# Scores and score maxima of two attention blocks in sixteen 32x32 parts of the array instead of four of 32x128

## The chip, the cores and the metric

The kernel runs on one core of one Trainium2 chip. The metric is the device time of one execution in microseconds (us), and lower is better. The reference gives the result in 32-bit floats; the kernel uses 32-bit matmuls for everything that enters the result and bf16 matmuls where only a maximum or a mask is wanted.

## The reference

Four stages, one after the other, on x of 4 batches x 512 rows x 256 features, with a context of 4 x 1601 x 256:

```
x = x + tanh(g_xattn[0]) * cross_attention(layernorm(x), ctx)          # 16 heads of 64, 1601 keys
x = x + tanh(g_ffn[0])  * attention_and_experts(layernorm(x))          # 16 heads of 16, 4 key heads, 512 keys
x = x + tanh(g_xattn[1]) * masked_attention(ctx, ctx, layernorm(x))    # 16 heads of 16, 1601 keys, masked
x = x + tanh(g_ffn[1])  * attention_plus_gated_experts(layernorm(x))   # 16 heads of 16, 512 keys
```

Each attention is a softmax over keys of query times key, and that softmax times values. The third stage adds a mask of -1e20 to the scores before the softmax:

```
energy = jnp.einsum('nqhd,nkhd->nhqk', q, k)
energy = jnp.where(mask == 0, jnp.float32(-1e+20), energy)
attn = jax.nn.softmax(energy / math.sqrt(EMBED), axis=3)
out = jnp.einsum('nhql,nlhd->nqhd', attn, v)
```

## The kernel before

The kernel calls the four stages blocks 1 to 4. Blocks 2, 3 and 4 have heads of 16 features. Such a head is laid out in a strip of 32 partitions (`PAD` = 32: one row for minus the maximum, 16 for the features, the rest zero), and a group is four heads, one strip each. There are 4 groups (`GROUPS`) in each of 4 batches.

For a group, these units of work follow each other:

- **Score maxima.** `max3` (block 3) and `maxb` (blocks 2 and 4) take a tile of 128 queries and two heads. Per head there is one bf16 matmul: its stationary operand is 32 rows (the strip) x 128 queries, its moving operand 32 rows x 401 keys (block 3) or 512 keys. The two heads lie in different row strips of the array and in different banks. VectorE then reduces both banks to maxima (L1679 for block 3, L1689 for blocks 2 and 4). Block 3 has 4 query tiles x 4 key chunks x 2 head pairs = 32 units a group, 512 in all, written at L1228. Block 4 has 8 units a group, 128 in all, written at L1240, as are those of block 2.
- **Scores.** `scoreb` takes a tile of 124 keys (block 3, 13 tiles) or 128 keys (blocks 2 and 4, 4 tiles), and all four heads of the group. Per head there is one 32-bit matmul at L1267: stationary 32 rows x 128 keys, moving 32 rows x 512 queries. The compiled program runs each 32-bit matmul as two passes, so that a unit has 8 MATMUL records. Heads 0 and 1 go to a first slot of two banks, heads 2 and 3 to a second one, which has its own wait (`second_free`). In block 3 two full-array bf16 matmuls lay the mask under heads 0 and 1 before (L1260), and two add it to heads 2 and 3 behind (L1273). ScalarE takes the exponentials of each slot (L1435). Block 3 has 208 such units, block 4 has 64, and block 2 has 64.
- **Values.** `pvb` (L1288) multiplies the exponentials by the values: per head one 32-bit matmul in two passes, stationary 124 or 128 rows x 32 columns, moving 512 queries. The four heads lie in different column strips.

Three slots of two banks (`ring`, `RING` = 3) hold everything but the sums over values. `pv` has two banks. The order of the units is fixed: eight streams are woven together by a written list of turns (`TURNS_1` for blocks 1 and 2, `TURNS_3` for blocks 3 and 4), and a planner (`Pace`) gives each unit its slot from costs written in the code. In the second weave the order alternates `max3`, `pvb`, `maxb` or an expert of block 4, `scoreb`. TensorE works through this one list. Each unit waits for its slot and its inputs through semaphores, and only the last matmul of a unit (and, in `scoreb`, the last one of head 1) counts up `tensor_done`.

Of the kernel before, what the change touches and what calls it, by code (L numbers as in the profile page):

```python
# [15 lines left out]
P = 128  # L16
BANK = 512
# [5 lines left out]
PAD = P // GROUP  # L23
# [4 lines left out]
CHUNK = 401  # L28
# [4 lines left out]
GROUPS = HEADS // GROUP  # L33
# [723 lines left out]
def flamingo(nc, t, out):  # L757
# [3 lines left out]
    with ctx:  # L761
# [166 lines left out]
        def key_columns(blk, g, k0):  # L928

            if blk == 3:  # L930
                return kq_3[:, (g % 2) * (CTX + S) + k0:(g % 2) * (CTX + S) + k0 + P]
            return keys_place(blk, g)[:, k0:k0 + P]

        def queries_place(blk, g):
            if blk == 3:
                return kq_3[:, (g % 2) * (CTX + S) + CTX:(g % 2 + 1) * (CTX + S)]
            if blk == 2:
                return kq_2[:, g * S:(g + 1) * S]
            return kq_4[:, (g % 2) * 2 * S:(g % 2) * 2 * S + S]
# [6 lines left out]
        def queries_low(blk, g):  # L946
            return {2: kq_2b[:, g * S:(g + 1) * S], 3: kq_3b[:, CTX + 1:CTX + 1 + S], 4: kq_4b[:, 0:S]}[blk]
# [30 lines left out]
        def head_bank(unit, h):  # L978
            return ring_t[:, bank_of[unit][h // 2], (h % 2) * BANK:(h % 2 + 1) * BANK]
# [94 lines left out]
        def _(pe):  # L1074
            past = Past(pe)
            past.wait_ge(*at("vector", "setup"))
            for unit in order:
# [9 lines left out]
                slot = None  # L1087
                if unit in bank_of:
                    for lane, other in plan.bank_free[unit]:
                        past.wait_ge(*at(lane, *other))  # L1090
                    slot = slot_tile(unit) if kind != "scoreb" else None
                if kind == "turn":
                    blk, b = a
                    xn = xn_a if blk == 1 else xn_of[blk] if blk in xn_of else src[:, b, :, :]
                    source = ("rms1", b) if blk == 20 else ("ln", blk, b)
                    for q in range(QT):
                        past.wait_ge(vector_done, plan.end["vector", source] - QT + 1 + q)
                        for f in range(FT):
                            last = pe.transpose(slot[:, f * S + q * P:f * S + (q + 1) * P], xn[:, q, f * P:(f + 1) * P], ident)
                    last.then_inc(tensor_done, 1)  # L1100
                elif kind == "kproj":
# [3 lines left out]
                    for j in range(2):  # L1105
                        c0 = CTX_CHUNKS[2 * c + j]
                        place = slot[:, j * BANK:j * BANK + CHUNK]
                        pe.matmul(place, pair_weights(p)[:, 1, 0, :], ctxT[:, 0, c0:c0 + CHUNK], start=True, stop=False)  # L1108
                        last = pe.matmul(place, pair_weights(p)[:, 1, 1, :], ctxT[:, 1, c0:c0 + CHUNK], start=False, stop=True)  # L1109
                    last.then_inc(tensor_done, 1)  # L1110
                elif kind == "qproj":
# [5 lines left out]
                              start=False, stop=True).then_inc(tensor_done, 1)  # L1117
                elif kind == "vproj":
                    b, p, j = a
                    for i, (k0, kn) in enumerate(CTX_TILES[8 * j:8 * j + 8]):  # L1120
                        place = slot[0:kn, i * P:(i + 1) * P]
                        pe.matmul(place, ctxT[:, 0, k0:k0 + kn], pair_weights(p)[:, 2, 0, :], start=True, stop=False)  # L1122
                        last = pe.matmul(place, ctxT[:, 1, k0:k0 + kn], pair_weights(p)[:, 2, 1, :], start=False, stop=True)  # L1123
                    last.then_inc(tensor_done, 1)
                elif kind == "maxa":
                    b, p, q, c = a
                    c0 = CTX_CHUNKS[c]
                    past.wait_ge(*at("vector", "qproj", b, p))
                    for h in range(2):
                        own = slice(64 * h, 64 * h + 64)  # L1130
                        last = pe.matmul(slot[:, h * BANK:h * BANK + CHUNK], queries_ab[own, q * P:(q + 1) * P],  # L1131
                                         keys_ab[own, c0:c0 + CHUNK], start=True, stop=True)
                    last.then_inc(tensor_done, 1)
                elif kind == "rowa":
                    b, p = a
                    past.wait_ge(*at("vector", "nega", b, p))
                    for q in range(QT):
                        last = pe.matmul(slot[:, q * P:(q + 1) * P], neg_cols_a[:, q, :], ident_b[:, :], start=True, stop=True)
                    last.then_inc(tensor_done, 1)
                elif kind == "scorea":  # L1140
                    b, p, k = a
                    k0, kn = CTX_TILES[k]
                    past.wait_ge(*at("scalar", "qproj", b, p))
                    past.wait_ge(*at("scalar", "rowa", b, p))
                    for h in range(2):
                        own = slice(64 * h, 64 * h + 64)
                        pe.matmul(slot[:, h * BANK:(h + 1) * BANK], select_b[own, :], neg_rows[own, p % 2, :], start=True, stop=False)  # L1147
                    for h in range(2):
                        own = slice(64 * h, 64 * h + 64)
                        last = pe.matmul(slot[0:kn, h * BANK:(h + 1) * BANK], keys_a[own, p % 2, k0:k0 + kn], queries_a[own, p % 2, :],  # L1150
                                         start=False, stop=True)
                    last.then_inc(tensor_done, 1)
                elif kind == "pva":
# [6 lines left out]
                    for h in range(2):  # L1160
                        last = pe.matmul(pv_a[64 * h:64 * h + 64, :], values_a[0:kn, p % 2, k, 64 * h:64 * h + 64],  # L1161
                                         exps_a[0:kn, slot_of["scorea", b, p, k], h * S:(h + 1) * S], start=k == 0, stop=k == NKT - 1)
# [26 lines left out]
                elif kind == "projqk":  # L1189
                    b, g = a  # L1190
# [31 lines left out]
                elif kind == "max3":  # L1222
                    b, g, q, hp, c = a
                    past.wait_ge(*at("dma", "load_low", b, g))
                    past.wait_ge(*at("vector", "low", b, g))
                    for i in range(2):
                        own = slice(PAD * (2 * hp + i), PAD * (2 * hp + i + 1))
                        last = pe.matmul(slot[:, i * BANK:i * BANK + CHUNK], queries_low(3, g)[own, q * P:(q + 1) * P],  # L1228
                                         keys_low(3, g)[own, CTX_CHUNKS[c]:CTX_CHUNKS[c] + CHUNK], start=True, stop=True)
                    last.then_inc(tensor_done, 1)  # L1230
                elif kind == "maxb":
# [3 lines left out]
                        past.wait_ge(*at("vector", "projq", b, g // 2))  # L1235
                    else:
                        past.wait_ge(*at("vector", "projqk", b, g))
                    for i in range(2):
                        own = slice(PAD * (2 * hp + i), PAD * (2 * hp + i + 1))
                        last = pe.matmul(slot[:, i * BANK:(i + 1) * BANK], queries_low(blk, g)[own, q * P:(q + 1) * P],  # L1240
                                         keys_low(blk)[own, :], start=True, stop=True)
                    last.then_inc(tensor_done, 1)
                elif kind == "rowb":
# [5 lines left out]
                elif kind == "scoreb":  # L1249
# [12 lines left out]
                    for h in range(GROUP):  # L1262
                        own = slice(PAD * h, PAD * h + PAD)
                        if h == 2:
                            for lane, other in plan.second_free[unit]:
                                past.wait_ge(*at(lane, *other))
                        last = pe.matmul(head_bank(unit, h), key_columns(blk, g, k0)[own, :],  # L1267
                                         queries_place(blk, g)[own, :], start=blk != 3 or h >= 2, stop=blk != 3 or h < 2)
                        if h == 1:
                            last.then_inc(tensor_done, 1)  # L1270
                    if blk == 3:
# [686 lines left out]
```

## Time and profile before

| what | value |
|---|---|
| three runs | 3416.55, 3425.77, 3425.16 us (median 3425.16) |
| span of the profiled execution, first to last instruction | 3413.1 us |
| TensorE busy | 3262.7 us (96%), 18335 MATMUL records |
| VectorE busy | 1980.1 us (58%) |
| ScalarE busy | 1437.7 us (42%) |
| GpSimd busy | 955.6 us (28%) |

The profiled execution has no time of its own beside its span; the three runs lie 3.5 to 12.7 us above the span, which leaves out what comes before the first and behind the last instruction. Busy TensorE time is from the start of a matmul to the modelled end of its results, and matmuls overlap in the array, so the 96% do not say that the array could take no more. What a unit costs is read from starts, not from busy times.

### The profile page before, as it was taken

Reading aid. Unit: us, or ns where it says so; the run is one execution under the profiler, and the core shown is the slowest. Engines: PE = TensorE matmul, PEld = TensorE weight load, DVE = VectorE, ACT = ScalarE, POOL = GpSimd, SP = SyncE. Lnnn points to the kernel's source line nnn. Section 1 sums busy time; section 2 is a strip of 40 time slices with the busy share of each in tenths; the row PEclk is TensorE's granted clock in tenths of the full one; section 3 lists DMA queues with packets and bytes.
Section 4 is the critical chain, followed back from the end, with each engine's and each line's share of the span. In section 5 each row is a group of like instructions: output and inputs, shape, how many; then the busy total and the mean of one; then the engine's idle time right before and its main releaser. Section 6 shows DMA issues by size and latency. Waiting matters only on the chain.

```text
span 3413.1 us, 45107 instructions
## 1 busy us (share of the span) xinstructions
PE 3262.7 (96%) x18335; PEld 1412.6 (41%) x18335; DVE 1980.1 (58%) x4290; ACT 1437.7 (42%) x1645; POOL 955.6 (28%) x469
## 2 busy tenths in 40 slices
PE   7999999999999999999997979899999999999999
PEld 3444444444434444444433752223333334333344
DVE  4444456554555546655574028677777676766446
ACT  3433444445434454344443213454444444545533
POOL 4655555654466444546300001000000000000000
PEclk9999999999999999999998989999999999999989
DMA  3000000000000000000031510211111111110000
GB/s 151 12 13 13 31 11 11 7 12 32 7 21 12 13 28 12 19 13 7 4 110 54 165 56 19 58 50 53 20 31 37 47 29 41 30 40 20 13 19 19
DMA packets 68249, 114.41 MB, mean 34 GB/s; under 512 B 4849, under 2 KB 49545, under 8 KB 67530
## 3 DMA queue, kind: packets, MB, share of 16 engines
q1 hardware_dynamic: 62666, 96.58, 8.9%
q0 software_dynamic: 5376, 14.95, 1.9%
q8 instruction: 144, 2.36, 0.3%
q14 instruction: 63, 0.52, 0.0%
HBM read 101.30 MB, written 16.78 MB: 35 GB/s over the span
## 4 chain that ended last, share of the span: by engine, by line
PE 85%; DVE 6%; ACT 4%; POOL 2%; DMA 1%; issue 1%; ACTq 0%; DVEq 0%; POOLq 0%
PE pv L1161 11%; PE ring L1267 10%; PE ring L1150 9%; PE pv L1288 9%; PE ring L1228 3%; PE ring L1260 3%; PE ring L1131 3%; PE ring L1122 3%; PE ring L1108 3%; PE ring L1147 3%; PE ring L1123 3%; PE ring L1109 2%; PE ring L1273 2%; ACT wide L1435 2%; PE ring L1345 2%; PE ring L1326 2%
## 5 line engine op out<-in xcount | busy, mean ns | idle before, releaser
L1532 POOL TENSOR_TENSOR wide<-wide 124x1024 f32<-124x1024 f32 (+1 forms) x341 | 803.6, 2357 | 180.1 <-ACT wide L1428 142.1
L1435 ACT ACTIVATE wide<-ring 124x1024 f32<-124x1024 f32 (+2 forms) x544 | 528.3, 1022 | 532.2 <-PE ring L1267 529.7
L1651 DVE TENSOR_REDUCE max_a<-ring 128x2 f32<-128x802 f32 x512 | 493.3, 990 | 395.9 <-PE ring L1131 395.6
L1428 ACT ACTIVATE wide<-ring 124x1024 f32<-124x1024 f32 (+1 forms) x416 | 425.0, 1026 | 438.3 <-PE ring L1150 386.0
L1679 DVE CUSTOM_DVE_ANT_0 rest<-ring,slim 128x401 bf16<-128x401 f32 x683 | 374.5, 575 | 119.4 <-PE ring L1228 113.5
L1150 PE MATMUL ring<-wide 64*124 64x512 f32 (+1 forms) x1664 | 424.8, 589 | 0.0
L1161 PE MATMUL pv<-wide 124*64 124x512 f32 (+1 forms) x1664 | 414.0, 613 | 8.2 <-ACT wide L1428 8.2
L1689 DVE TENSOR_REDUCE slim<-ring 128x2 f32<-128x1024 f32 x256 | 307.9, 1221 | 111.2 <-PE ring L1240 109.4
L1267 PE MATMUL ring<-slim 32*128 32x512 f32 x2176 | 350.5, 641 | 3.4 <-ACT wide L1435 2.7
L1502 POOL DMA_DIRECT2D slim<-in_ctx_k x16 | 8.9, 560 | 988.4 <-PE ring L1228 938.0
L1529 POOL TENSOR_TENSOR wide<-wide 124x1024 f32<-124x1024 f32 x31 | 73.0, 2355 | 600.4 <-ACT wide L1428 587.0
L1679 DVE CUSTOM_DVE_ANT_0 slim<-ring,slim 128x401 bf16<-128x401 f32 x341 | 195.7, 574 | 67.1 <-PE ring L1228 65.5
L1288 PE MATMUL pv<-wide,slim 124*32 124x512 f32 (+1 forms) x1664 | 223.4, 610 | 0.2 <-ACT wide L1435 0.2
L1161 PEld LDWEIGHTS pv<-wide 124*64 124x64 f32 (+1 forms) x1664 | 99.3, 136 | 229.7 <-issue 201.9
L1150 PEld LDWEIGHTS ring<-wide 64*124 64x124 f32 (+1 forms) x1664 | 155.5, 183 | 72.9 <-issue 50.4
L1228 PE MATMUL ring<-slim 32*128 32x401 bf16 x1024 | 159.7, 341 | 21.2 <-ACT wide L1435 11.9
L1267 PEld LDWEIGHTS ring<-slim 32*128 32x128 f32 x2176 | 112.3, 184 | 133.4 <-issue 104.8
L1147 PE MATMUL ring<-wide,select_b 64*128 64x512 bf16 x832 | 158.9, 379 | 8.1 <-ACT wide L1428 6.1
L1131 PE MATMUL ring<-wide 64*128 64x401 bf16 x1024 | 155.7, 337 | 9.5 <-DVE max_a L1651 4.5
L1122 PE MATMUL ring<-wide 128*124 128x128 f32 (+1 forms) x832 | 162.1, 276 | 0.4 <-DVE max_a L1651 0.4
L1123 PE MATMUL ring<-wide 128*124 128x128 f32 (+1 forms) x832 | 160.4, 273 | 0.0
L1435 ACT ACTIVATE slim<-ring 128x1024 f32<-128x1024 f32 x128 | 124.4, 1021 | 75.4 <-PE ring L1267 75.0
(241 smaller groups left out, 3992.1 us busy)
## 6 DMA issues: line engine op xcount, KB each, us to landing
slim<-in_ctx_k SPq DMA_DIRECT2D x16, 800.5 KB, 4.4
wide<-in_w_pair SPq DMA_DIRECT2D x32, 384.0 KB, 3.1
slim<-in_ctx_v SPq DMA_DIRECT2D x16, 744.0 KB
wide<-in_w SPq DMA_DIRECT2D x16, 512.0 KB, 4.9
wide<-in_we SPq DMA_DIRECT2D x16, 512.0 KB, 3.7
wide<-in_ctxT SPq DMA_DIRECT2D x4, 1601.0 KB, 7.0
slim<-in_ctx_k POOLq DMA_DIRECT2D x16, 400.2 KB, 4.7
wide<-padded_x SPq DMA_DIRECT2D x8, 640.0 KB, 5.2
```

Source lines behind the costliest of these rows:

```text
L1122: pe.matmul(place, ctxT[:, 0, k0:k0 + kn], pair_weights(p)[:, 2, 0, :], start=True, stop=False)
L1123: last = pe.matmul(place, ctxT[:, 1, k0:k0 + kn], pair_weights(p)[:, 2, 1, :], start=False, stop=True)
L1150: last = pe.matmul(slot[0:kn, h * BANK:(h + 1) * BANK], keys_a[own, p % 2, k0:k0 + kn], queries_a[own, p % 2, :], start=False, stop=True)
L1161: last = pe.matmul(pv_a[64 * h:64 * h + 64, :], values_a[0:kn, p % 2, k, 64 * h:64 * h + 64], exps_a[0:kn, slot_of["scorea", b, p, k], h * ...
L1267: last = pe.matmul(head_bank(unit, h), key_columns(blk, g, k0)[own, :], queries_place(blk, g)[own, :], start=blk != 3 or h >= 2, stop=blk ...
L1288: last = pe.matmul(pv_of[blk][PAD * h:PAD * h + PAD, :], value_columns(blk, g, k, kn, h), exps_tile(blk, b, g, k, h)[0:kn, :], start=k == ...
L1428: sc.activation(exps_a[0:kn, slot_of[unit], :], slot[0:kn, :], ACT.Exp, scale=WIDE ** -0.5).then_inc(scalar_done, 1)
L1435: sc.activation((exps_2 if blk == 2 else exps_34)[0:kn, first + 2 * i:first + 2 * i + 2, :].rearrange("p h n -> p (h n)"), ring_t[0:kn, ba ...
L1532: po.tensor_tensor(sums[0:kn, :], sums[0:kn, :], view, ALU.add).then_inc(pool_done, 1)
L1651: ve.reduce_max(max_a[:, :, q, c], slot.rearrange("p (h n) -> p h n", h=2)[:, :, 0:CHUNK], AX.X).then_inc(vector_done, 1)
L1679: ve.tensor_tensor_reduce(out=max_junk[junk], in0=slot[:, i * BANK:i * BANK + CHUNK], in1=maskQ_sb[:, q, CTX_CHUNKS[c]:CTX_CHUNKS[c] + CHUNK],
L1689: ve.tensor_reduce(neg_cols[blk][:, q, 2 * hp * PAD:2 * hp * PAD + PAD + 1:PAD], slot.rearrange("p (h n) -> p h n", h=2), AX.X, ALU.max, n ...
```

## The change

In block 3 and block 4 each matmul of `scoreb` and of the maxima is cut into four along its 128 stationary columns. Each part has 32 rows and 32 columns, writes 32 partitions of the same bank, and streams the same moving operand as the others of its head. Block 2 keeps matmuls of 32x128. Data, order of the units, slots, waits and semaphore counts stay as they were. In the `scoreb` of block 2 the loop runs once.

```
                 elif kind == "max3":
...
-                    for i in range(2):
+                    for i, j in product(range(2), range(GROUPS)):
                         own = slice(PAD * (2 * hp + i), PAD * (2 * hp + i + 1))
-                        last = pe.matmul(slot[:, i * BANK:i * BANK + CHUNK], queries_low(3, g)[own, q * P:(q + 1) * P],
+                        last = pe.matmul(slot[j * PAD:(j + 1) * PAD, i * BANK:i * BANK + CHUNK],
+                                         queries_low(3, g)[own, q * P + j * PAD:q * P + (j + 1) * PAD],
                                          keys_low(3, g)[own, CTX_CHUNKS[c]:CTX_CHUNKS[c] + CHUNK], start=True, stop=True)
                     last.then_inc(tensor_done, 1)
                 elif kind == "maxb":
...
-                    for i in range(2):
-                        own = slice(PAD * (2 * hp + i), PAD * (2 * hp + i + 1))
-                        last = pe.matmul(slot[:, i * BANK:(i + 1) * BANK], queries_low(blk, g)[own, q * P:(q + 1) * P],
+                    for i, j in product(range(2), range(1 if blk == 2 else GROUPS)):
+                        own, wide_part = slice(PAD * (2 * hp + i), PAD * (2 * hp + i + 1)), P if blk == 2 else PAD
+                        c0 = j * wide_part
+                        last = pe.matmul(slot[c0:c0 + wide_part, i * BANK:(i + 1) * BANK],
+                                         queries_low(blk, g)[own, q * P + c0:q * P + c0 + wide_part],
                                          keys_low(blk)[own, :], start=True, stop=True)
                     last.then_inc(tensor_done, 1)
...
-                        last = pe.matmul(head_bank(unit, h), key_columns(blk, g, k0)[own, :],
-                                         queries_place(blk, g)[own, :], start=blk != 3 or h >= 2, stop=blk != 3 or h < 2)
+                        wide_part = P if blk == 2 else PAD
+                        for c0 in range(0, P, wide_part):
+                            last = pe.matmul(head_bank(unit, h)[c0:c0 + wide_part, :], key_columns(blk, g, k0)[own, c0:c0 + wide_part],
+                                             queries_place(blk, g)[own, :], start=blk != 3 or h >= 2, stop=blk != 3 or h < 2)
                         if h == 1:
                             last.then_inc(tensor_done, 1)
```

## Rows read from the trace of the kernel before

**Rows 1.** The profile's page: busy time, granted clock in 40 slices, chain by engine
```profile
PE 3262.7 (96%) x18335; PEld 1412.6 (41%) x18335; DVE 1980.1 (58%) x4290; ACT 1437.7 (42%) x1645; POOL 955.6 (28%) x469
...
PEclk9999999999999999999998989999999999999989
...
PE 85%; DVE 6%; ACT 4%; POOL 2%; DMA 1%; issue 1%; ACTq 0%; DVEq 0%; POOLq 0%
```

**Rows 2.** Windows by stage: stretch, length, busy us of each engine, clock, DMA
```profile
0.00:1940.00 1940.00, 1859.99 (x10212) 872.48 (x10213) 1022.19 (x1452) 809.02 (x955) 916.06 (x422) 0.98 0.09 31
2040.00:3200.00 1160.00, 1122.39 (x6681) 384.18 (x6680) 829.06 (x2611) 530.27 (x574) 31.66 (x39) 0.98 0.14 35
```

**Rows 3.** Groups of TensorE instructions from 2075 us to the end
```profile
L1267 PE MATMUL ring<-slim 32*128 32x512 f32 x1664 | 268.3, 643 | 2.7 <-ACT wide L1435 2.7
L1288 PE MATMUL pv<-wide,slim 124*32 124x512 f32 (+1 forms) x1664 | 223.4, 610 | 0.2 <-ACT wide L1435 0.2
L1228 PE MATMUL ring<-slim 32*128 32x401 bf16 x960 | 148.8, 342 | 20.6 <-ACT wide L1435 11.9 <-DVE max_b L1679 5.5 <-DVE slim L1710 1.5
...
L1267 PE MATMUL ring<-wide 32*128 32x512 f32 x512 | 82.6, 638 | 2.0 <-ACT wide L1457 0.9 <-DVE max_b L1679 0.5 <-DVE wide L1704 0.2
```

**Rows 4.** Chain of waits, 2600 to 2640 us: first and last of eight L1267 pieces
```profile
2601.31 1.47 PE ring L1267 x8
...
2610.20 1.07 PE ring L1267 x8
...
2635.49 1.40 PE ring L1267 x8
```

**Rows 5.** Timeline, second weave: start us, length, engine, line
```profile
2600.70 0.61 PE L1260 MATMUL ring<-slim,ident_b 124*128 124x512 bf16 x2
...
2601.24 1.54 PE L1267 MATMUL ring<-slim 32*128 32x512 f32 x8
...
2602.71 0.61 PE L1273 MATMUL ring<-slim,ident_b 124*128 124x512 bf16 x2
...
2603.25 0.34 PE L1228 MATMUL ring<-slim 32*128 32x401 bf16 x2
...
2603.52 1.06 PE L1288 MATMUL pv<-wide,slim 124*32 124x512 f32 x8
...
2604.52 0.59 PE L1228 MATMUL ring<-slim 32*128 32x401 bf16 x6
...
2610.13 1.14 PE L1267 MATMUL ring<-slim 32*128 32x512 f32 x8
```

**Rows 6.** Timeline of TensorE, window 2604.4 to 2604.6 us
```profile
2603.98 0.61 PE L1288 MATMUL pv<-wide,slim 124*32 124x512 f32 x4
2604.52 0.35 PE L1228 MATMUL ring<-slim 32*128 32x401 bf16 x4
```

**Rows 7.** Instructions of single lines: duration ns min/median/max
```profile
L1267 PE MATMUL ring<-slim x2176: 587/588/1218, 523.3 to 3265.7; 32*128 32x512 f32 x198
...
L1288 PE MATMUL pv<-wide,slim x1664: 590/594/1063, 2086.4 to 3273.5; 124*32 124x512 f32 x170, 113*32 113x512 f32 x15
...
L1228 PE MATMUL ring<-slim x1024: 325/339/513, 2042.1 to 3195.5; 32*128 32x401 bf16 x171
```

**Rows 8.** Timeline of TensorE: neighbours of two shapes in blocks 1 and 2
```profile
946.60 1.02 PE L1150 MATMUL ring<-wide 64*124 64x512 f32 x4
947.55 0.87 PE L1240 MATMUL ring<-slim 32*128 32x512 bf16 x4
...
703.02 1.08 PE L1161 MATMUL pv<-wide 124*64 124x512 f32 x4
704.03 1.06 PE L1288 MATMUL pv<-slim 128*32 128x512 f32 x8
```

**Rows 9.** Timeline of TensorE, 1384.8 to 1385.2 us: first and last of 14 short matmuls
```profile
1384.84 0.17 PE L1334 MATMUL ring<-chosen_b,earlier_b 128*128 128x8 bf16 x1
...
1385.17 0.17 PE L1337 MATMUL ring<-before_b,ones_b 128*128 128x8 bf16 x1
```

## The prediction

> **What bounds the kernel now.** I read the page first. TensorE is busy for 96% of the span, the next engine, VectorE, for 58%, and 85% of the chain that ended last is TensorE's [rows 1]. The clock row is nearly all 9s: outside the gap between the two weaves the granted clock is the upper level, 2.4 GHz, and the change leaves no longer pauses, so I count no clock effect. The windows place the change. Blocks 3 and 4 fill the time from 2040 us to the end; up to 3200 us TensorE is busy for 1122 of 1160 us, VectorE for 829 and ScalarE for 530 [rows 2]. The groups from 2075 us on show that TensorE hardly waits in front of the changed lines: 2.7 and 2.0 us ahead of the scores, 20.6 us ahead of the block 3 maxima [rows 3]. In this stage a nanosecond added between two matmul starts is therefore paid almost in full, and one saved is kept almost in full.
>
> Busy time says little of a unit's cost, since a matmul's record holds a tail that overlaps the next one. I read starts. A merged row of the timeline gives its first start and its length; the length less one matmul's own duration is the time from first to last start.
>
> **How an unchanged scores unit runs.** The undisturbed unit is eight records in 1.14 us [rows 5]; one lasts 0.588 us [rows 7], so the last starts 0.55 us after the first. A 512-column bf16 matmul takes 0.61 - 0.39 = 0.22 us of starts (the mask pair at 2600.70 [rows 5]); a pass of a 32-bit matmul takes two of those, 0.43 us, as the pair of 64-row heads at 946.60 shows (1.02 - 0.59) [rows 8]. So the L1267 unit has 0.12 us beside its pass. Four starts of L1288 lie in 0.61 - 0.594 = 0.02 us, 0.0065 us apart [rows 6, 7]; four heads take 0.02 us of the 0.12. The other 0.10 us is the load of the second pass's 128 weight columns, which is not hidden here. L1288, with 32 columns, has 1.06 - 0.594 = 0.47 us from first to last start [rows 5, 7]: 0.02 of starts and 0.03 of load. L1161, with 64 columns, lies between [rows 8].
>
> **What the change costs, part by part.**
>
> 1. *Scores, 208 + 64 = 272 units (1664/8 and 512/8 records [rows 3]).* Removed: 128-column loads; added: 24 more records and as many loads a unit. If sixteen parts load side by side, as L1288's four column parts and L1267's four row strips do, the exposed load falls from 0.10 to 0.03 us. The starts grow from three intervals to fifteen, 15 x 0.0065 = 0.10 us in place of 0.02. Last start: 0.43 + 0.03 + 0.10 = 0.56 us against 0.55. I take the unit as unchanged. No row shows 32x32 parts. The load is bounded by zero (the 946.60 row exposes none) and by four loads one after the other in a strip, 4 x 0.03 = 0.11 us: -0.03 to +0.08 us a unit, -8 to +22 us in all. A unit's 32 matmuls and 32 loads must also be fed in one go, and the rows show bursts of eight only. I add 0.01 us a unit, 3 us, for feeding, with 0 below.
>
> 2. *Scores whose second half waits.* Of eight L1267 pieces of the chain between 2600 and 2640 us three take 1.07 us and five longer, up to 1.51 [rows 4]; the 1.54 us unit at 2601.24 is such a one, its heads 2 and 3 waiting for their slot [rows 5]. There the end is the second half's start plus its own length, which falls from 0.54 us (0.43 + 0.10 + one interval) to 0.43 + 0.03 + 7 x 0.0065 = 0.50. With half of 272 units: 136 x 0.04 = -5.5 us. A gain of nothing is the other bound.
>
> 3. *Maxima, 512 + 128 = 640 units.* The four starts of L1228 at 2604.52 lie in 0.35 - 0.339 = 0.01 us, some 0.0035 us apart [rows 6, 7]. Eight starts in place of two put the last one 6 x 0.0035 = 0.02 us later, and what comes behind in another shape waits for the last. In the cycle shown L1228 is followed by L1288 0.27 us after its start [rows 5], so this is on the path. Full count: 640 x 0.02 = +13 us. Some units overlap with another of the same shape or wait for a slot, so I take two thirds, +9 us. At the spacing of the 32-bit starts it would be 640 x 0.04 = +25 us.
>
> 4. *Maxima in the same strips again.* In the six-record row at 2604.52 the third pair starts 0.59 - 0.34 = 0.25 us after the first [rows 5], where 401 columns at 2.4 GHz are 0.17: 0.08 us of load is exposed, and 0.03 would be left. I estimate 50 such places, since most units come singly or as the two different head pairs: -2.5 us.
>
> 5. *Changes of shape.* L1260's second matmul starts at 2600.92 (2600.70 + 0.61 - 0.39) and streams for 0.21 us, the next shape starts at 2601.24: 0.1 us is left, and every change in the rows costs about that: full array to 32x128 [rows 5], 32x128 to 128x32 (0.27 less 0.17), 128x32 back, 64x128 to 32x128 and 128x64 to 128x32 [rows 8]. The last two keep the column or the row division and pay all the same. 32x32 beside 128x32 keeps the column division, so I expect 0.1 us there too, and no number of changes differs: block 3 and 4 have no 32x128 left beside.
>
> 6. *The others.* VectorE learns of its maxima 0.02 us later; it has slack [rows 2]. ScalarE may start heads 0 and 1 about 0.04 us sooner. DMA and its queues are untouched; SyncE's and GpSimd's reloads wait for the last maxima, whose drift is part of the sum.
>
> The Trainium skill speaks against the maxima's edit: "TensorEngine Tiling (Array Packing)", Restrictions and Gotchas, says that column tiling shuts off the fast weight load, which bf16 weights of 128 columns otherwise have. By that rule and the page "TensorE: Matmul & The Clock Gate" (LDWEIGHTS), 32 columns would load in an estimated 0.027 us against 0.08 in the row; the rule then costs nothing, unless the four loads queue (0.11), where term 4 would turn from -2.5 to +1.5 us.
>
> **Sum.** 0 + 3 - 5.5 + 9 - 2.5 = +4 us on a span of 3413.1. The runs lie 3.5 to 12.7 us above that span, their median 12.1; moved to the median, 3425.2 + 4 = **3429 us**. That is within 0.3% (10 us), about what a measurement of this kernel can tell from no change.
>
> **Rivals.**
>
> - *Loads of a strip's parts queue* (slower). In favour: no row shows more than four loads at once, and each strip has one stream of partitions. Against: L1288 loads four column parts together over all rows. Term 1 becomes +22, term 2 about zero, term 4 +1.5: 22 + 3 + 9 + 1.5 = +35 us, 3460. Chance 0.13.
> - *Too many parts for what can wait* (slower). A second pass waits in front of the next head's first pass in the program. With 16 parts, if only eight second passes can be held, heads 2 and 3 start when the first pass of 0 and 1 ends: +0.43 us where the second half doesn't wait anyway, 136 to 272 units, +58 to +117 us, 3490 to 3545. It decides from the ninth part on. L1267's row of eight shows that four can be held. Chance 0.07.
> - *Issue becomes the bound* (slower). Fourteen short matmuls start 0.33/13 = 0.025 us apart [rows 9]. Were that the price of each small matmul, a scores unit would need 32 x 0.025 = 0.80 us (+0.25, 67 us) and a maxima unit 0.17 more (110 us): about 3605. For scores it decides from 0.55/32 = 0.017 us a record. Against: parts start 0.0035 and 0.0065 us apart when in different tiles [rows 6]. Chance 0.04. The skill's "TensorE: Matmul & The Clock Gate", Back-to-back issue gap, has the same 25 ns as floor and, in one setting of the decoder, some 62 ns a matmul; the 0.025 us row and the closer starts speak against the latter.
> - *Going to and from the values becomes cheap* (faster), because 32x32 and 128x32 divide the columns alike. 2176/8 = 272 values units, entered and left: at most 544 x 0.1 = 54 us; with most neighbours of these shapes, 45 us less: 3384. Against it the changes in [rows 8]. Chance 0.10.
> - *The second pass's load vanishes*, as in the 64-row strips: 0.03 x 272 = 8 us less and the halves 4 us less: -8 us, 3417. Chance 0.10.
>
> **Chances and range.** The forecast has 0.56 and its own range is 3419 to 3441 (term 3 from two thirds to the wide spacing, feeding 0 to 6 us, term 2 absent or there). Faster by over 0.3%: 0.10 + 0.06 of the last rival + 0.03 of the forecast's low end = 0.19. Slower: 0.13 + 0.07 + 0.04 + 0.13 of the forecast's upper end = 0.37. Within: 0.44. The range runs from the cheap change of shape to the queued loads, 3380 to 3462, and leaves out some 0.12 above.
>
> **What would show it.** In the profile after: undisturbed scores units still near 1.14 us from first start to last end, and a first-to-second-pass distance of 0.46 us in place of 0.53 (queued loads: 0.53 or more; too many parts: heads 2 and 3 starting 0.43 us late). L1228 to L1288 0.29 us in place of 0.27. L1288 to the next shape still 0.1 us beyond its stream. The records of L1228 and L1267 four times as many. The prediction is wrong if sixteen parts don't stream together, which no row can tell, or if a change of shape is priced by more than the rows show.

## The result and the profile after

The changed kernel takes 3435.51 us, the median of 7 runs (3428.97 to 3438.61); the kernel before took 3425.16 us in 7 runs beside it (3416.55 to 3430.69). The ratio is 1.0034 with a 95% interval of 1.0023 to 1.0045. On 3425.16 us that is +11.6 us, between +8 and +15: slower. Whether it lies beyond the 0.3% that I took as the bound can't be told: the interval includes it, and the medians are 10.35 us apart, which is 0.30%. The profiled execution took 3428.97 us, its span 3426.8. Of the executions below, one of e7 and one each of the kernel before beside e5 to e7 and beside e8 and e9 fell into a much slower state of the chip and count in no figure.

The page of the kernel after. Against [rows 1] TensorE has 10,347 matmul records more and about the same busy time, and the clock row is again nearly all 9s:

```profile
PE 3270.1 (95%) x28682; PEld 1390.7 (41%) x28703; DVE 1982.4 (58%) x4290; ACT 1436.6 (42%) x1645; POOL 955.3 (28%) x469
...
PEclk9999999999999999999988989999999999999999
...
PE 85%; DVE 6%; ACT 4%; POOL 2%; issue 1%; DMA 1%; ACTq 0%; POOLq 0%; DVEq 0%
```

The windows of the stages in the kernel after, columns as in [rows 2]:

```profile
0.00:1940.00 1940.00, 1859.26 (x10195) 872.91 (x10204) 1023.06 (x1452) 808.71 (x955) 915.96 (x422) 0.98 0.09 31
2040.00:3200.00 1160.00, 1118.15 (x15756) 359.40 (x15762) 822.90 (x2586) 523.25 (x567) 31.64 (x39) 0.99 0.14 36
```

The first stretch is as before. In the second, VectorE does 2586 instructions where it did 2611 and ScalarE 567 where it did 574: the same length of time holds less work. The groups of TensorE from 2075 us on, kernel after. L1267 has become L1272, L1288 is L1293, L1240 is L1242, L1260 is L1263 and L1273 is L1278. ScalarE's L1435 is now L1440, and VectorE's L1679 and L1689 are L1684 and L1694:

```profile
L1272 PE MATMUL ring<-slim 32*32 32x512 f32 x6656 | 264.7, 606 | 2.8 <-ACT wide L1440 2.8
L1293 PE MATMUL pv<-wide,slim 124*32 124x512 f32 (+1 forms) x1664 | 223.1, 609 | 0.2 <-ACT wide L1440 0.2
L1228 PE MATMUL ring<-slim 32*32 32x401 bf16 x3872 | 162.9, 341 | 23.7 <-ACT wide L1440 14.7 <-DVE max_b L1684 6.0 <-DVE slim L1715 1.5
...
L1272 PE MATMUL ring<-wide 32*32 32x512 f32 x2048 | 81.9, 599 | 2.1 <-ACT wide L1462 0.9 <-DVE max_b L1684 0.5 <-ACT wide L1440 0.3
...
L1242 PE MATMUL ring<-wide 32*32 32x512 bf16 x1024 | 52.0, 395 | 4.2 <-DVE slim L1694 1.4 <-ACT wide L1440 1.1 <-DVE wide L1771 1.0
```

Set against [rows 3], the scores' busy time fell (268.3 to 264.7 and 82.6 to 81.9 us) and the maxima's rose (148.8 to 162.9 us). The idle time ahead of L1228 rose from 20.6 to 23.7 us.

The timeline of TensorE in the second weave, kernel after:

```profile
2604.33 0.60 PE L1263 MATMUL ring<-slim,ident_b 124*128 124x512 bf16 x2
2604.86 1.14 PE L1272 MATMUL ring<-slim 32*32 32x512 f32 x32
2605.93 0.60 PE L1278 MATMUL ring<-slim,ident_b 124*128 124x512 bf16 x2
2606.46 0.36 PE L1228 MATMUL ring<-slim 32*32 32x401 bf16 x8
2606.76 1.07 PE L1293 MATMUL pv<-wide,slim 124*32 124x512 f32 x8
2607.75 0.36 PE L1228 MATMUL ring<-slim 32*32 32x401 bf16 x8
2608.03 0.41 PE L1242 MATMUL ring<-wide 32*32 32x512 bf16 x8
...
2612.17 0.65 PE L1228 MATMUL ring<-slim 32*32 32x401 bf16 x24
```

Narrow windows of the same timeline, around 2605.58 us and up to 2605.25 us. They cut the 32 records into their two passes, second pass first:

```profile
2605.31 0.69 PE L1272 MATMUL ring<-slim 32*32 32x512 f32 x16
...
2604.86 0.71 PE L1272 MATMUL ring<-slim 32*32 32x512 f32 x16
```

The weight loads (PEld) of the same unit, kernel after:

```profile
2604.85 0.23 PEld L1272 LDWEIGHTS ring<-slim 32*32 32x32 f32 x32 [0.42 <-issue]
```

and the loads, the first pass and the second pass of the undisturbed unit in the kernel before:

```profile
2610.13 0.31 PEld L1267 LDWEIGHTS ring<-slim 32*128 32x128 f32 x8 [0.42 <-issue]
...
2610.13 0.71 PE L1267 MATMUL ring<-slim 32*128 32x512 f32 x4
...
2610.66 0.61 PE L1267 MATMUL ring<-slim 32*128 32x512 f32 x4
```

What the reader is to see here:

- The undisturbed scores unit lasts 1.14 us with 32 records, as it did with 8 [rows 5]. Its second pass starts 2605.31 - 2604.86 = 0.45 us after the first. All sixteen second passes lie in the first row, so its sixteen starts take 0.69 - 0.588 = 0.10 us, 0.0065 us apart.
- The load that the unit waits for is that of its first pass. The loads of both passes end at 2604.85 + 0.23 = 2605.08 us, 0.23 us before the second pass starts, and in the kernel before at 2610.44, 0.22 us before. It is the first pass whose records are longer: 0.71 - 0.02 = 0.69 us with 128 columns and 0.71 - 0.10 = 0.61 with 32, against 0.588 in the second pass. Their starts are recorded together with their loads, and the difference, 0.10 and 0.02 us, is what the load holds up.
- L1228 to L1293 takes 2606.76 - 2606.46 = 0.30 us, in place of 0.27 [rows 5]. The unit's own row grew from 0.34 to 0.36 us: that is the 0.02 us of later last start, and it comes out again behind the unit.
- Three maxima units in a row take 0.65 us in place of 0.59 [rows 5]. That is 0.06 us more for three units, and nothing came back.
- L1293 to the next L1228 takes 0.99 us, as L1288 to L1228 did before (1.00 us [rows 5]), although both now have column parts of 32.

Single instructions of L1228 in the kernel after (duration in ns, min/median/max):

```profile
L1228 PEld LDWEIGHTS ring<-slim x4096: 86/88/98, 2044.0 to 3207.9; 32*32 32x32 bf16 x196
L1228 PE MATMUL ring<-slim x4096: 324/339/513, 2044.1 to 3207.9; 32*32 32x401 bf16 x196
```

The pieces of the chain of waits at L1272, kernel after, 2600 to 2640 us:

```profile
2604.93 1.07 PE ring L1272 x32
...
2608.98 1.43 PE ring L1272 x27
...
2637.50 1.07 PE ring L1272 x32
```

Four of its eight pieces take 1.07 us, the length that the undisturbed unit had in [rows 4]; the long one shown takes 1.43 us, where the same unit took 1.47 before.

**Where the 11.6 us arise.** I compared the starts of the same instructions in the two traces. The changed kernel is 2.0 us late when the second weave begins, 4.0 us at 2133 us, 8.1 at 2637, 11.8 at 3142 and 13.7 at the end: the loss grows through the whole second weave. The 2.0 us arise before it, where TensorE's matmuls are those of the kernel before. Taken unit by unit, from a unit's first start to that of the next unit, the second weave says who pays. The 512 `max3` units cost +15.9 us and the 128 block 4 `maxb` units +2.2. The 208 `scoreb` units of block 3 cost -3.7 and the 64 of block 4 -0.7. Everything else comes to -2, and the sum is +11.7. It is the 13.7 us between two single executions less those 2.0; that it meets the 11.6 of the runs is chance. What is firm in it is the small, regular part. Of the 18.1 us at the maxima, 13.4 are shifts of at most 0.15 us. In 357 places a maxima unit stands alone between units of other kinds; the median shift there is +0.021 us, and only 3% of them move by less than 0.008 us. The other 5 us are single longer steps. Those come and go from one execution to the next: the traces of e1 and e4 to e7 below, whose maxima are whole as before, have 2 to 10 us more than before at the same units.

### The profile page after: what moved, and what is told of

Read it like the earlier page. It is cut to its first block, busy times and chain, and to the rows that moved or that the text cites. A ratio compares the mean times of both kernels' runs of the same rounds, so it can differ in the third digit from the quotient of the medians.

```text
span 3426.8 us, 65822 instructions
## 1 busy us (share of the span) xinstructions
PE 3270.1 (95%) x28682; PEld 1390.7 (41%) x28703; DVE 1982.4 (58%) x4290; ACT 1436.6 (42%) x1645; POOL 955.3 (28%) x469
## 4 chain that ended last, share of the span: by engine, by line
PE 85%; DVE 6%; ACT 4%; POOL 2%; issue 1%; DMA 1%; ACTq 0%; POOLq 0%; DVEq 0%
PE pv L1161 11%; PE ring L1272 10%; PE ring L1150 9%; PE pv L1293 9%; PE ring L1228 4%; PE ring L1263 3%; PE ring L1131 3%; PE ring L1122 3%; PE ring L1108 3%; PE ring L1147 3%; PE ring L1123 3%; PE ring L1109 2%; PE ring L1278 2%; ACT wide L1440 2%; PE ring L1350 2%; PE ring L1242 2%
## 5 line engine op out<-in xcount | busy, mean ns | idle before, releaser
L1440 ACT ACTIVATE wide<-ring 124x1024 f32<-124x1024 f32 (+2 forms) x544 | 527.5, 1021 | 543.4 <-PE ring L1272 541.7
L1684 DVE CUSTOM_DVE_ANT_0 rest<-ring,slim 128x401 bf16<-128x401 f32 x683 | 375.3, 576 | 124.4 <-PE ring L1228 121.6
L1694 DVE TENSOR_REDUCE slim<-ring 128x2 f32<-128x1024 f32 x256 | 308.1, 1222 | 115.7 <-PE ring L1242 113.4
L1272 PE MATMUL ring<-slim 32*32 32x512 f32 (+1 forms) x7168 | 349.1, 609 | 3.1 <-ACT wide L1440 2.8
L1684 DVE CUSTOM_DVE_ANT_0 slim<-ring,slim 128x401 bf16<-128x401 f32 x341 | 196.0, 575 | 71.0 <-PE ring L1228 70.9
L1293 PE MATMUL pv<-wide,slim 124*32 124x512 f32 (+1 forms) x1664 | 223.1, 609 | 0.2 <-ACT wide L1440 0.2
L1228 PE MATMUL ring<-slim 32*32 32x401 bf16 x4096 | 173.5, 341 | 24.1 <-ACT wide L1440 14.7
L1228 PEld LDWEIGHTS ring<-slim 32*32 32x32 bf16 x4096 | 56.6, 88 | 274.7 <-ACT wide L1440 137.8
L1440 ACT ACTIVATE slim<-ring 128x1024 f32<-128x1024 f32 x128 | 124.2, 1021 | 78.1 <-PE ring L1272 77.7
```

What stands on the lines that cost most here:

```text
L1228: last = pe.matmul(slot[j * PAD:(j + 1) * PAD, i * BANK:i * BANK + CHUNK], queries_low(3, g)[own, q * P + j * PAD:q * P + (j + 1) * PAD], ...
L1272: last = pe.matmul(head_bank(unit, h)[c0:c0 + wide_part, :], key_columns(blk, g, k0)[own, c0:c0 + wide_part], queries_place(blk, g)[own, : ...
L1293: last = pe.matmul(pv_of[blk][PAD * h:PAD * h + PAD, :], value_columns(blk, g, k, kn, h), exps_tile(blk, b, g, k, h)[0:kn, :], start=k == ...
L1440: sc.activation((exps_2 if blk == 2 else exps_34)[0:kn, first + 2 * i:first + 2 * i + 2, :].rearrange("p h n -> p (h n)"), ring_t[0:kn, ba ...
L1684: ve.tensor_tensor_reduce(out=max_junk[junk], in0=slot[:, i * BANK:i * BANK + CHUNK], in1=maskQ_sb[:, q, CTX_CHUNKS[c]:CTX_CHUNKS[c] + CHUNK],
L1694: ve.tensor_reduce(neg_cols[blk][:, q, 2 * hp * PAD:2 * hp * PAD + PAD + 1:PAD], slot.rearrange("p (h n) -> p h n", h=2), AX.X, ALU.max, n ...
```

## The experiments

Each kernel differs from the kernel before only in the width of the parts. The diff of e1 is against the kernel before; each later one is against the kernel told just before it. In the maxima only the line of block 3 is shown, and block 4's `maxb` is given the same width. e1:

```
-                    for i in range(2):
+                    for i, c0 in product(range(2), range(0, P, P)):
...
-                        last = pe.matmul(head_bank(unit, h), key_columns(blk, g, k0)[own, :],
...
+                        wide_part = {2: P, 3: PAD, 4: PAD}[blk]
+                        for c0 in range(0, P, wide_part):
+                            last = pe.matmul(head_bank(unit, h)[c0:c0 + wide_part, :], key_columns(blk, g, k0)[own, c0:c0 + wide_part],
...
```

e1 to e4 ran on one chip (before: 3420.52 us there), e5 to e7 on a second one (3432.9), e8 and e9 on a third (3428.5).

### e1: the scores in 32x32, the maxima whole

> Scores of blocks 3 and 4 in 32x32 parts, all maxima in 32x128 as before. Theory A (starts 0.0035 and 0.0065 us apart against weight loads of columns/1.2 GHz): the 272 scores units give back what the trace after shows for them, 0.02 us each on average, -4.4 us; but in block 4 a scores unit now has another shape than the maxima beside it, and the order has 70 such neighbours, each 0.10 to 0.17 us dearer, +7 to +12 us. Net +3 to +8 us against before, ratio 1.001 to 1.002. Theory B (sixteen parts are what costs: 24 more records a unit): +9 us or more from the scores alone, with the neighbours +16 to +21 us, ratio 1.005 or more.

Measured: 3422.53 us, ratio 1.0005 (0.9996 to 1.0014). The scores' edit doesn't carry the loss. The result lies below the range of either theory, 1.001 to 1.002 for A and 1.005 or more for B; its interval reaches into A's. The timeline of e1, a block 4 scores unit and the maxima behind it:

```profile
2630.37 1.16 PE L1272 MATMUL ring<-wide 32*32 32x512 f32 x32
2631.46 0.34 PE L1228 MATMUL ring<-slim 32*128 32x401 bf16 x2
```

and of the kernel after, the same two units:

```profile
2634.22 1.16 PE L1272 MATMUL ring<-wide 32*32 32x512 f32 x32
2635.20 0.47 PE L1228 MATMUL ring<-slim 32*32 32x401 bf16 x8
```

With two shapes the maxima start 1.09 us after the scores, with one shape 0.98 us. A change of shape behind the scores costs 0.1 us here too, though both shapes divide the rows into the same strips.

### e2: the maxima in 32x32, the scores whole

```
-                    for i, c0 in product(range(2), range(0, P, P)):
+                    for i, c0 in product(range(2), range(0, P, PAD)):
...
-                        wide_part = {2: P, 3: PAD, 4: PAD}[blk]
+                        wide_part = {2: P, 3: P, 4: P}[blk]
```

> Maxima of blocks 3 and 4 in 32x32 parts, all scores in 32x128 as before. Theory A: 640 units whose last start is 0.021 us later, +13 us, up to the +18 us that the trace after shows at these units, and 70 neighbours of another shape, +7 to +12 us: +20 to +30 us, ratio 1.006 to 1.009. Theory B (the scores carry the loss): the neighbours alone, +7 to +12 us, ratio 1.002 to 1.0035.

Measured: 3438.95 us, ratio 1.0046 (1.0032 to 1.0060), +16 us. The ratio missed both ranges: it lies between Theory B's 1.002 to 1.0035 and Theory A's 1.006 to 1.009, and its interval overlaps the two. With e1 beside it, the loss sits in the maxima all the same. What Theory A had too high is the price of the neighbours. e1 and e2 together cost 17.5 us, the whole change 11.6, and each of the two has the 70 neighbours of two shapes once. So the 6 us between them are twice their price: 3 us, 0.04 us at each place, where 0.10 to 0.17 was expected. The traces show why. Compared start by start, the step out of a block 4 scores unit into maxima (47 places) is 0.08 to 0.1 us longer than before in both kernels, the step into one (23 places) 0.00 to 0.05. The intervals leave room for nothing and for twice as much.

### e3: everything in two parts of 32x64

```
-                    for i, c0 in product(range(2), range(0, P, PAD)):
+                    for i, c0 in product(range(2), range(0, P, 2 * PAD)):
...
-                        wide_part = {2: P, 3: P, 4: P}[blk]
+                        wide_part = {2: P, 3: 2 * PAD, 4: 2 * PAD}[blk]
```

> Scores and maxima of blocks 3 and 4 in two parts of 32x64 a head. Theory A: a maxima unit's last start is 2 x 0.0035 = 0.007 us later, 640 units +4.5 us; a scores unit has 0.43 + 0.053 + 7 x 0.0065 = 0.53 us from first to last start against 0.555, -0.027 us, and a waiting second half 0.50 against 0.54, -0.04 us, 272 units -9 us. Net -3 to -5 us, ratio 0.9985 to 0.999. If each added record costs more than its start spacing: slower than before.

Measured: 3425.15 us, ratio 1.0015 (1.0005 to 1.0026). This missed: I had expected a gain. The single instructions of L1228 in e3:

```profile
L1228 PEld LDWEIGHTS ring<-slim x2048: 100/101/124, 2044.6 to 3209.0; 32*64 32x64 bf16 x187
L1228 PE MATMUL ring<-slim x2048: 325/353/540, 2044.7 to 3209.0; 32*64 32x401 bf16 x187
```

and its timeline:

```profile
2608.79 0.36 PE L1228 MATMUL ring<-slim 32*64 32x401 bf16 x4
2609.08 1.07 PE L1293 MATMUL pv<-wide,slim 124*32 124x512 f32 x8
```

Two parts have two late starts a unit instead of six, 0.007 us, and yet L1293 starts 0.29 us after L1228, 0.02 more than before. The rest is in the load. A bf16 load of 64 columns takes 101 ns, where one of 32 takes 88 in the kernel after and one of 128 takes 91, as e4 shows, whose maxima are whole:

```profile
L1228 PEld LDWEIGHTS ring<-slim x1024: 89/91/101, 2045.7 to 3193.1; 32*128 32x128 bf16 x171
```

and the median matmul behind the 64-column load takes 353 ns in place of 339. Those 0.014 us in 640 units are 9 us. Put into the expected sum, they turn -3 to -5 us into +4 to +6, which is what e3 showed (+5 us). The traces agree: start by start, a maxima unit that stands alone is 0.020 us later than before with two parts, as it is with four, and the shifts of at most 0.15 us come to -8 us over the scores units.

### e4 and e7: only the scores of block 3, in two parts of 32x64

```
-                    for i, c0 in product(range(2), range(0, P, 2 * PAD)):
+                    for i, c0 in product(range(2), range(0, P, P)):
...
-                        wide_part = {2: P, 3: 2 * PAD, 4: 2 * PAD}[blk]
+                        wide_part = {2: P, 3: 2 * PAD, 4: P}[blk]
```

The maxima are whole again. In block 3 the scores stand between the two full-array mask pairs, so no change of shape is added.

> Only the scores of block 3 in two parts of 32x64 a head, all else as before; the mask matmuls on both sides of a unit are of another shape in any case. Theory A: 208 units at -0.027 (undisturbed) or -0.04 us (second half waits): -6 to -8 us, ratio 0.998. If parts as such cost, no gain: 1.000 or above.

> The kernel of e4 once more beside the two others (only the scores of block 3, in two parts of 32x64): -6 to -8 us, ratio 0.998. A ratio of 1.000 would say that the first one was chance.

Measured: 3411.56 us, ratio 0.9980 (0.9968 to 0.9993), and on the second chip 3429.22 us, 0.9977 (0.9964 to 0.9991). By these ratios the kernel is faster than the one before, by a quarter of a per cent. The chain of waits in e4:

```profile
2611.61 1.04 PE ring L1272 x16
...
2615.28 1.04 PE ring L1272 x16
...
2627.72 1.07 PE ring L1272 x8
```

The undisturbed unit takes 1.04 us in two parts. The last row is a block 4 unit, not split, with its 1.07 us. The gain at the units is firm: compared start by start with the kernel before, the 208 units are 0.028 us shorter in the median, and their shifts of at most 0.15 us come to -7.1 us in e4's trace and to -7.2 in e7's.

The gain in the runs is less firm than its intervals look, because part of it is the clock. e7's executions fall into two groups, five at 3416 to 3422 us with a mean granted clock of 0.977 to 0.980 and six at 3429 to 3434 us with 0.973 to 0.975. Within the executions of one kernel, 0.001 less of mean clock goes with some 2.6 us more time (an estimate from the runs of all kernels here; 2.1 to 3.0 in each alone). The means of e4 and e7 lie 7 us below those of the kernel before, and their mean clocks, 0.9787 against 0.9776 and 0.9760 against 0.9745, stand for some 3 and 4 us of that. Some 3 to 4.5 us are left. Whether the higher clock is chance or comes with the kernel is not shown.

### e5: only the scores of block 3, in four parts of 32x32

```
-                        wide_part = {2: P, 3: 2 * PAD, 4: P}[blk]
+                        wide_part = {2: P, 3: PAD, 4: P}[blk]
```

> Only the scores of block 3 in 32x32 parts, all else as before. Theory A (a unit's length beside its pass is the weight load of its columns plus the starts): undisturbed units 0.003 us shorter, those with a waiting second half 0.04 us, on average the 0.02 us seen in the trace after: 208 units -4 us, ratio 0.9985 to 0.9995, between before and the two-part version, whose undisturbed units are 0.03 us shorter. Theory B (the added records cost): 1.000 or above.

Measured: 3434.94 us, ratio 1.0002 (0.9992 to 1.0011). The small gain that I had expected was not there, or too small to be told, and 1.0002 is what Theory B had said. The traces speak for Theory A at the units: compared start by start with the kernel before, the shifts of at most 0.15 us at the 208 units come to -4.5 us. But the mean of e5's runs lies 9 us above that of e7's, on the same chip and at the same mean clock of 0.976, where the units account for 3. In the two traces e5 falls 7 us behind e7 between 2040 and 2340 us, in single steps of up to 5 us. Why is open, and so it is not shown that the added records cost nothing.

### e6: the scores of blocks 3 and 4 in two parts

```
-                        wide_part = {2: P, 3: PAD, 4: P}[blk]
+                        wide_part = {2: P, 3: 2 * PAD, 4: 2 * PAD}[blk]
```

> Scores of blocks 3 and 4 in two parts of 32x64, maxima as before. Against the version with block 3 alone (ratio 0.998): 64 units of block 4 give -2 us, and 70 neighbours of another shape cost 0.08 us each, +5.6 us: +3.6 us, ratio 0.999. If a change between parts and whole strips were free, it would be 0.9975.

Measured: 3425.07 us, ratio 0.9983 (0.9971 to 0.9996). It can't be told from e7. Where the maxima stayed whole, scores in two parts gained each time (e4, e6, e7), and scores in four parts neither time (e1, e5), with the reserve about the clock told under e4.

### e8: the whole change without the scores of block 3

```
-                    for i, c0 in product(range(2), range(0, P, P)):
+                    for i, c0 in product(range(2), range(0, P, PAD)):
...
-                        wide_part = {2: P, 3: 2 * PAD, 4: 2 * PAD}[blk]
+                        wide_part = {2: P, 3: P, 4: PAD}[blk]
```

> The change without its edit of the scores of block 3: maxima of blocks 3 and 4 and scores of block 4 in 32x32 parts, so no neighbours of a new shape. Theory A: 640 maxima units, +13 to +18 us, block 4's scores -1 us: +12 to +17 us, ratio 1.0035 to 1.005, as slow as the whole change or slower. Theory B (the scores of block 3, 208 of 272 units and most added records, carry the loss): the loss goes away, 1.000 to 1.001.

Measured: 3443.28 us, ratio 1.0042 (1.0029 to 1.0055), +14 us. With the change undone in the scores that do most of the work, the loss stays and seems 3 us larger: block 3's scores gave a little back in the whole change, as term 2 has it. The intervals of the two overlap.

### e9: e8 with the scores of block 3 in two parts

```
-                        wide_part = {2: P, 3: P, 4: PAD}[blk]
+                        wide_part = {2: P, 3: 2 * PAD, 4: PAD}[blk]
```

> The whole change, with the scores of block 3 in two parts of 32x64 instead of four of 32x32. Theory A: against e8 the two-part scores give -6 to -8 us: +6 to +9 us against before, ratio 1.0018 to 1.0026. If the parts' gain depended on whole-strip maxima around them, it would stay at e8's ratio.

Measured: 3444.59 us, ratio 1.0048 (1.0035 to 1.0062). This missed too: e4's gain should have come on top of e8. Unit by unit the gain is there. The steps at `scoreb` of block 3 are 3.4 us shorter in e9's trace than in e8's, and all shifts of at most 0.15 us come to -5.0 us. Fewer, larger shifts put +4.8 us back.

One of them stands out: a wait of TensorE for VectorE's layernorm, 10.5 - 6.2 = 4.3 us more in e9. The waits of TensorE between 2040 and 2340 us (in total, times, longest) in e9:

```profile
PE ring L1099 <- DVE wide L1638: 10.5, 2, 6.2
...
PE ring L1263 <- ACT wide L1440: 1.1, 2, 0.6
```

and in e8:

```profile
PE ring L1099 <- DVE wide L1638: 6.2, 1, 6.2
...
PE ring L1263 <- ACT wide L1440: 3.4, 3, 2.2
```

It did not eat the gain, since other waits were shorter: all rows of this view add up to 33.0 us in e9 and 32.5 in e8. By starts, e9 is 2.3 us behind e8 at 2040 us and 0.3 behind at 2340, so that it gains 2 us in this stretch. The clock doesn't tell the two apart there either. The windows, with the granted clock as the third column from the right, of e9 and e8:

```profile
2040.00:2340.00 300.00, 270.48 (x2930) 72.17 (x2930) 213.94 (x780) 120.45 (x128) 26.70 (x30) 0.93 0.17 45
...
2040.00:2340.00 300.00, 273.34 (x2515) 78.01 (x2516) 212.19 (x773) 120.25 (x128) 27.04 (x30) 0.93 0.17 45
```

A mean of 0.93 over 300 us means that 0.07 x 300 / 0.5 = 42 of them went by at the lower level, 1.2 GHz, in both. The gain is lost behind it. Between 2400 and 2440 us e9 falls 4.4 us behind. The windows of e9 and e8:

```profile
2400.00:2440.00 40.00, 38.47 (x380) 15.80 (x388) 27.98 (x77) 14.22 (x18) 0.56 (x1) 0.87 0.20 49
...
2400.00:2440.00 40.00, 38.35 (x414) 16.05 (x406) 31.47 (x89) 16.23 (x20) 0.56 (x1) 1.00 0.21 53
```

Here e9 had 0.13 x 40 / 0.5 = 10 us at the lower level and e8 none. TensorE is busy for 38 of the 40 us, so this can cost up to 5 us. The six runs of each say the same as a whole: e9's mean clocks are 0.971 to 0.974, e8's 0.974 to 0.977. By the 2.6 us for 0.001 told under e4, e9's lower clock stands for some 6 us, and at e8's clock it would be some 4 us faster than e8 where it was 2 us slower in the mean. By this estimate the gain of the two parts is there, and the lower clock outweighs it. Why all six runs of e9 had the lower clock is open.

One kernel on two chips shows how far a stretch can differ. Windows of e4 and of e7, which is the same kernel:

```profile
2040.00:2340.00 300.00, 276.67 (x2044) 73.50 (x2044) 222.59 (x803) 126.05 (x134) 26.94 (x30) 0.96 0.18 48
...
2040.00:2340.00 300.00, 269.91 (x1971) 70.37 (x1972) 216.58 (x790) 123.09 (x131) 26.93 (x30) 0.94 0.17 46
```

## Why the prediction came near, and the term that was too small

The forecast was 3429 us with a range of 3380 to 3462; measured were 3435.51. The direction of the sum and the range were right. The loss was +11.6 us in place of +4, at the edge of the 0.3% that the likeliest case allowed. The mechanism was that of the forecast but for the place of one load, and none of the rivals came true.

- **Term 3, the maxima's later last start, was the mis-sized one.** Predicted were +13 us at full count, taken at two thirds, +9. The size per unit was right, 0.021 us against 0.02. The step that failed is "Some units overlap with another of the same shape or wait for a slot, so I take two thirds": practically all pay, and the regular shifts of the 640 units come to +13.4 us. Units that wait for their slot pay as well. Where VectorE sets the cycle (one maxima unit after another between 2044 and 2077 us), the median cycle grew from 1.03 to 1.05 us. The timeline there shows how. Kernel before:

```profile
2056.47 0.34 PE L1228 MATMUL ring<-slim 32*128 32x401 bf16 x2
...
2056.86 0.58 DVE L1679 CUSTOM_DVE_ANT_0 rest<-ring,slim 128x401 bf16<-128x401 f32 x1
```

Kernel after:

```profile
2057.07 0.36 PE L1228 MATMUL ring<-slim 32*32 32x401 bf16 x8
...
2057.50 0.58 DVE L1684 CUSTOM_DVE_ANT_0 rest<-ring,slim 128x401 bf16<-128x401 f32 x1
```

VectorE's reduction starts 0.05 and 0.07 us after the last matmul has ended, so that a later end moves it. With the single longer steps the count at the maxima is +18.1 us in this pair of traces; the idle time ahead of L1228, 23.7 us against 20.6 [rows 3], holds 3 of those, and what the steps owe to the change is not shown. e2 (+16 us with the maxima alone) and e8 (+14 us) bear out that the maxima carry the loss.
- **Term 4, the same strips again, did not appear.** Its -2.5 us rested on a load of 0.08 us falling to 0.03. The third unit of a triple should have started earlier; instead the triple takes 0.65 us in place of 0.59. A bf16 load of 32 columns takes 88 ns, one of 128 columns 91, so there was no shorter load to be had.
- **Term 1, the unchanged scores unit, held in its sum, with one load in the wrong place.** 1.07 us in the chain before and after. The second pass starts 0.45 us after the first, where 0.46 was predicted. The load of 32 columns and sixteen starts 0.0065 us apart add up as foreseen. But the prediction calls the exposed load that of the second pass. By the records it is that of the first: both passes' loads have ended 0.2 us before the second pass starts, and it is the first pass that lasts 0.69 us with 128 columns and 0.61 with 32. The sum stayed right because either place gives the same time from first start to last. The 3 us for feeding 32 records were not needed.
- **Term 2, the waiting second half, held.** Predicted -5.5 us, measured -4.4 over all 272 units, and one long unit fell from 1.47 to 1.43 us. e8, without block 3's part, agrees in sign.
- **Term 5, the change of shape, held.** 0.99 against 1.00 us from L1293 to L1228, and e1 showed 0.1 us between 32x32 and 32x128 as well. In the whole change the number of such places didn't grow.
- **Term 6 and the clock.** The stretch from 2040 to 3200 us has 0.99 against 0.98 [rows 2] in single executions. The whole change's loss is not a clock effect in the profiled pair, whose mean clock is 0.979 in both; the clocks of the other runs of the kernel before are not on record. But "I count no clock effect" was too sure for differences of 5 us, as e7 and e9 show.

With the regular shifts alone the sum is 0 - 4.4 + 13.4 = +9 us, inside the +8 to +15 of the runs. With all steps of the second weave in this pair of traces it is -4.4 + 18.1 - 2 = +11.7 us; that one adds up by construction.

Of the rivals, queued loads would have put the second pass 0.53 us or more behind the first; it is 0.45. Too many parts would have started heads 2 and 3 of an undisturbed unit 0.43 us late; all sixteen first passes start within 0.10 us, and the unit kept its 1.14. An issue bound of 0.025 us a record would have made 0.80 us of 32 records, and they start within 0.55 us. The cheap way to and from the values would have shown between L1293 and L1228. Had the load vanished, 0.43 us would lie between the passes, and it is 0.45.

The Trainium skill's "TensorEngine Tiling (Array Packing)", Restrictions and Gotchas, says that column tiling shuts off the fast weight load. I had weighed this and priced it at nothing. For four parts that was so (88 ns against 91). For two parts it was not: e3's 101 ns for 64 columns, more than 128 columns need, agrees with the rule.

What stays open: what decides how long TensorE is at 1.2 GHz, in e9's runs and between 2040 and 2340 us, why e5 is 9 us slower than e7, and where the 2 us before the second weave come from. No kernel was tried that changes the stretch from 2040 to 2340 us by itself, nor the maxima in parts that are written in another order.

## What to carry to other kernels

Splitting the columns of these matmuls, whose heads already fill all four row strips, added no throughput. It traded a shorter exposed weight load against more starts, 0.0065 us each for 32-bit and 0.0035 us for bf16 matmuls, so look first for whether a load is exposed at all. Here it was in front of the first pass of the 32-bit matmuls, where two parts are the best compromise (1.04 us a unit against 1.07 for one and for four), and in the short bf16 maxima the parts only delayed what came next. When a dense engine has hundreds of small equal units on its path, count a delay in full for all of them; waits that look like cover may belong to a cycle that lengthens with the unit. And when kernels differ by less than 0.3%, compare the mean granted clock of all their executions before reading a ratio: a clock lower by 0.001 went with some 2.6 us here, as much as a third of what e4 gained.

## What I had not expected of the hardware

- Sixteen 32x32 parts stream side by side, with 0.45 us from pass to pass against 0.53 for four of 32x128, and a start costs the same whether 4 or 16 of them are under way (0.0065 us, 32-bit).
- A bf16 load of 64 columns takes longer (101 ns) than one of 128 columns (91 ns) or of 32 (88 ns), and it delays the matmul behind it by 14 ns.
- 24 more matmuls and 24 more loads left the undisturbed scores unit as long as it was: 32 matmuls and 32 loads were fed in 0.55 us.
- Of a 32-bit matmul's two loads only that of the first pass holds it up: 0.10 us with 128 columns, 0.05 with 64 (first passes of 0.64 us in e4) and 0.02 with 32.
- One kernel, timed on two chips, had a granted clock of 0.96 and of 0.94 in the same 300 us, and profiled executions of 3410.18 and 3433.60 us. Part of that is the chip, whose kernel before differed by 12 us as well.
